# Two attention steps swapped on the matrix engine: new scores ahead of the older unit's probabilities times values

## The reference

```
x = x + tanh(g_xattn) * attention(layernorm(x), ctx)      # 16 heads of 64, causal
x = x + tanh(g_ffn)   * ffn(layernorm(x))                 # quantised gate/up/down products

attention(q, ctx):  qh, kh, vh = split_heads(q @ Wq, ctx @ Wk, ctx @ Wv)
                    p = softmax(mask(qh @ kh^T / 8));  out = (p @ vh) @ Wo + bo
```

## Time and profile before

| | before |
|---|---|
| three runs, median (lowest to highest) | 1842.2 us (1840.18 to 1842.58) |
| the profiled execution, its own time | 1842.63 us |
| its span from first to last instruction | 1840.6 us |
| PE busy in the span | 1722.7 us (94%) |
| DVE busy | 1375.7 us (75%) |
| ACT busy | 1128.3 us (61%) |
| POOL busy | 427.1 us (23%) |
| mean granted PE clock | 0.984 of full speed |

### The profile page before, as it was taken

The page is one execution under the profiler, slowest core; times in us unless marked ns, Lnnn a source line. Parts: engine busy times, 40 slices in busy tenths (PEclk is TensorE's granted clock), DMA queues, the critical chain, the costliest instruction groups (busy, mean ns, idle before and its releaser), DMA issues. The chain is left out here.

```text
span 1840.6 us, 36804 instructions
## 1 busy us (share of the span) xinstructions
PE 1722.7 (94%) x12200; PEld 1452.0 (79%) x12200; DVE 1375.7 (75%) x2260; ACT 1128.3 (61%) x3073; POOL 427.1 (23%) x373
## 2 busy tenths in 40 slices
PE   6899999999999999999999999959997887997998
PEld 5788888888888888888888887848885665786998
DVE  6667667677676676776766768758888998998785
ACT  4656566556566565565665655646656887664665
POOL 2222313323223232232232322210002332431000
PEclk9999999999999999999999999989998998998999
DMA  5010001000010011010100010016774563334664
GB/s 183 13 37 25 23 24 44 26 24 34 28 32 23 24 35 34 24 34 20 40 23 24 34 36 12 24 64 231 261 253 151 182 185 99 129 135 153 210 202 148
DMA packets 58600, 151.14 MB, mean 82 GB/s; under 512 B 4416, under 2 KB 33728, under 8 KB 56640
## 3 DMA queue, kind: packets, MB, share of 16 engines
q1 hardware_dynamic: 58560, 150.62, 24.3%
HBM read 85.07 MB, written 65.54 MB: 82 GB/s over the span
## 5 line engine op out<-in xcount | busy, mean ns | idle before, releaser
L320 POOL TENSOR_TENSOR prob<-prob,rsums 128x512 f32<-128x512 f32 x256 | 261.1, 1040 | 755.3 <-DVE rsums L497 755.3
L357 ACT ACTIVATE prob<-masked,neg_max 128x128 f32<-128x128 f32 x1024 | 396.0, 391 | 7.2 <-DVE neg_max L463 3.8
L368 ACT ACTIVATE qT<-proj 128x512 f32<-128x512 f32 x128 | 76.6, 598 | 260.9 <-PE proj L606 260.9
L479 DVE COPY probT<-trans 128x512 f32<-128x512 f32 x128 | 88.3, 690 | 152.6 <-PE trans L641 148.8
L357 ACT ACTIVATION_READ_ACCUMULATOR prob<-masked,neg_max 128x1 f32 x1024 | 195.6, 191 | 0.0
L463 DVE TENSOR_REDUCE neg_max<-masked 128x4 f32<-128x512 f32 x256 | 175.7, 686 | 8.8
L461 DVE TENSOR_TENSOR masked<-score,mask_add 128x512 f32<-128x512 f32 x256 | 174.1, 680 | 1.4 <-PE score L666 0.6
L758 PE MATMUL pair<-xThi,wup_hi 128*128 128x512 f32 x360 | 144.7, 402 | 28.4 <-POOL xTlo L1232 16.9
L641 PE MATMUL trans<-ident,prob 128*128 128x128 f32 x1024 | 153.3, 272 | 1.6 <-ACT probT L377 1.6
L677 PE MATMUL y<-wo_hi,o_hi 128*128 128x256 f32 x512 | 147.3, 288 | 3.6 <-DVE o_lo L503 3.6
L485 DVE COPY v_sb<-proj 128x512 f32<-128x512 f32 x128 | 88.5, 691 | 80.7 <-PE proj L606 80.0
(11 more groups left out here) (190 smaller groups left out, 4503.6 us busy)
## 6 DMA issues: line engine op xcount, KB each, us to landing
gate<-gate_d SPq DMA_DIRECT2D x30, 768.0 KB, 4.2
gate_d<-stage SPq DMA_DIRECT2D x8, 1536.0 KB, 6.0
n_u_d<-w_raw SPq DMA_DIRECT2D x16, 768.0 KB, 3.6
stage<-n_u_d SPq DMA_DIRECT2D x16, 768.0 KB, 5.9
gate_d<-gate SPq DMA_DIRECT2D x7, 1536.0 KB, 6.0
x_in<-in_x SPq DMA_DIRECT2D x16, 512.0 KB, 3.9
ctx_in<-in_ctx SPq DMA_DIRECT2D x16, 512.0 KB, 3.6
x_d<-x SPq DMA_DIRECT2D x16, 512.0 KB, 4.5
```

The costliest lines, as they stand in the source:

```text
L320: gp.tensor_tensor(pr, pr, rsums[:, h, :].rearrange("p (b o) -> p b o", o=1).broadcast_to([P, NB, P]), ALU.mult).then_inc(normed, 1)
L357: nc.scalar.activation(prob[:, c % 2, h, b, :], masked[:, h, b, :], ACT.Exp, bias=neg_max[:, h, b:b + 1], accum_out=psums[:, h, b:b + 1]). ...
L479: nc.vector.tensor_copy(probT[:, 1], trans[:]).then_inc(probT_copied[1], 1)
```

## The change

In PE's step, points 7 and 8 change places. Nothing else moves: the same instructions, waits and buffers, and the queues of ACT, DVE, POOL and SP keep their order.

```
@@ -718,10 +718,10 @@
                         value(g, i, n)
                 if nxt:
                     transpose_in(g, *ts[3])
+                if new:
+                    scores(g, c, u)
                 if old:
                     times_v(u - 2, co)
-                if new:
-                    scores(g, c, u)
 
             for n in range(2 * KC):
                 transpose_in(-1, first_job(n), n)
```

## The result

The changed kernel takes **1892.8 us** (median of four runs, 1888.83 to 1893.66) against 1841.6 before (four runs, 1840.18 to 1842.58): 1.0269 times as long, 95% interval 1.0255 to 1.0283. The forecast was 1879 with a range of 1870 to 1891, so the sign and the cause came out as written and the size did not: 51 us where the sum said 37. The profiled execution took 1893.66 us; its span is 1891.6, 51.0 more than before.

What follows compares the result with a forecast made beforehand. PE's queue was taken to bound the kernel. Fourteen repeated groups at 2.15 us (30.1) plus 6.5 for groups 0 and 15 gave 36.6 on 1842.63, so 1879 us, range 1870 to 1891.

Steps and rivals of the forecast that it cites:

- a stage is as long as PE's queue: Attention: PE is busy 94% of the span, so a change counts by what it does to that queue's waits.
- Earlier scores help nobody: Scores end 1.03 us earlier, but DVE's masks hardly wait for them; rival that this makes it faster, 1827, chance 0.04.
- The lateness of times_v: Each swapped unit: times_v ends 1.09 us later, delaying o_hi, o_lo and everything behind o_lo in DVE's queue.
- The seams at nothing: PE's switches between array splits around the two blocks: price taken as nothing, bounded at 7.6 us either way.
- xn at 1.37, not held: Unit 7: xn takes 1.37 us, not 2.06, as POOL is done; rival that the hold stays, 1889, chance 0.09.
- The clock at 1.00 in the repeated groups: Middle groups keep full clock; rival that new waits lower it in 15 groups, 24 us more, 1903, chance 0.07.
- no new wait is longer than about 1.5: Argument against the clock falling: PE's new waits stay at most about 1.5 us, against 3.4 where it fell.
- The late y: Units 1 to 5: the output projection's first weight load loses its head start, 0.07 us in each.
- PE's reaction to kT: Units 5 and 6: PE sees kT's end 0.05 us later; scores wait 0.57 and 1.00 us.
- The cover of unit 0: Unit 0: o_lo stands behind DVE's input copies, which hide the delay, so late y costs nothing there.
- its term: Unit 7: the first input transpose, waiting for xn, starts 1.87 us later, the total loss of units 5 to 7.
- Groups 0 and 15: Less slack because DVE also carries feed-forward weights: one and a half repeated groups, 3.2 us each, 6.5 together.

Runs made afterwards that it cites:

- e4: The swap only in units 5 and 6, the old order in all other units; 1866.7 us, 1.0132 of the kernel before.
- e3: The changed kernel with both layernorm statistics moved from behind o_lo to behind the masks of the next step; 1881.9 us, 1.021 of the kernel before.
- e11: The changed kernel with ACT's copy to kT ahead of head 0's four exponentials in units 5 and 6; 1874.7 us, 1.0181 of the kernel before.
- e9: The kernel before, unswapped, with earlier normalisation and the second layernorm's statistics in a DVE pause of unit 4; 1825.7 us, 0.991 of the kernel before.
- e10: The changed kernel with e9's moves, y behind the key projection and the masks' waits first in scores; 1835.2 us, 0.9956 of the kernel before.
- e2: The swap only in units 0 to 3 and 7, the old order in units 4 to 6; 1856.3 us, 1.0074 of the kernel before.
- e7: The changed kernel with the output projection (y) moved behind the key projection in units 0 to 5; 1884.2 us, 1.0224 of the kernel before.
- e1: The changed kernel with the masks' waits in scores put ahead of those for qT and kT; 1887.1 us, 1.0247 of the kernel before.

## Why the prediction was wrong in size and right in kind

**What held.** Steps that the runs bear out: a stage is as long as PE's queue. Earlier scores help nobody. The lateness of times_v reaches o_hi, o_lo, the statistics behind it, the masks, the exponentials, kT and then PE; e4 shows that it comes from the unit before, e3 that the statistics are a link of it, e11 that kT's place behind the exponentials is one. The seams at nothing: e9 and e10. xn at 1.37, not held: the changed trace, and POOL's pair ended 0.19 us ahead of xn. That was near the other way: in e3 and e11, where the pair overlaps xn again, the hold is back at 0.73 and 0.82. The clock at 1.00 in the repeated groups: the changed trace. The reason given for it, that no new wait is longer than about 1.5, did not hold in group 15, where kT kept PE for 2.35 us and the clock fell for 3.41. The late y at the start of units 1 to 5: e2 and e7.

**The term that failed first: PE's reaction to kT.** "PE sees it at 515.20 (0.05)" took the delay of a single wait, about what the transposes of unit 7 have (0.06). Behind the blocked wait of `scores` stand further entries, and each took about 0.1 us: 0.23 in unit 5 and 0.33 in unit 6 instead of 0.05. Units 5 and 6 came out 0.17 and 0.28 longer than predicted (0.81 for 0.64, 1.28 for 1.00), 14 x 0.45 = 6.3 us. e1, which moves the waits and nothing else, gave 0.17 and 0.19 of it back, 4.9 us in fourteen groups.

**The second: the late y.** It was put at 0.07 in units 1 to 4 and at nothing in unit 0, "which hide the delay". It measured 0.10, 0.09, 0.16 and 0.09 there, and 0.10 in unit 0, so 0.54 per group instead of 0.28: 14 x 0.26 = 3.6 us. e7 took the whole 0.54 away. The 0.09 to 0.10 is the load without its head start: the second matmul of y starts 0.21 us after the first and not 0.12. The 0.16 of unit 3 looks like the work of the residual, which stands ahead of o_lo on DVE in unit 2, but the rows of the changed kernel say otherwise:

```profile
506.19 1.40 DVE L562 SCALAR_TENSOR_TENSOR x<-y,tg,xres 128x512 f32<-128x512 f32 x2
...
508.34 0.69 DVE L503 TENSOR_TENSOR o_lo<-pv,o_hi 128x512 fp32r<-128x512 f32 x1 [0.60 <-ACT o_hi L395]
...
509.18 0.36 PE L677 MATMUL y<-wo_hi,o_hi 128*128 128x256 f32 x1
```

The residual ends at 507.59, and DVE then waits 0.60 us for o_hi; o_lo starts 1.77 us after its times_v (506.57), as in the other units. What unit 3 has more is a second wait in front of y (`wait_x1`): PE passes the wait for o_lo at 509.072, 0.04 after its end, and the load, which carries the other wait, starts at 509.149, 0.12 after o_lo's end, where it is 0.05 in unit 5 (526.88 to 526.93). So these 0.07 us are the first term's kind again, an entry more behind the blocked one.

The cover of unit 0, the input copies, was argued and not read from a row.

**The rest.** Unit 7 is 0.04 over its term (0.27 for 0.23), 0.6 us in all. Groups 0 and 15 cost 7.7 us and not 6.5; up to 1.7 of the 5.1 in group 15 are the 3.41 us at half clock, which the sum did not have. The 3.0 us behind the last q were not in the sum; 1.1 of them are the attention's own tail, up to 1.0 are more time at half clock, and whether these 1.0 and the 0.9 that are left belong to the change stays open, since the feed-forward stages vary by more. Together 6.3 + 3.6 + 0.6 + 1.2 + 3.0 = 14.7, against 51.0 - 36.6 = 14.4 that were missing (the unit medians are rounded).

**The range** ended at 1891 because it priced only what could go wrong with the seams, with xn and with two groups. The two terms that were off, 0.05 and 0.07, had no second value beside them: they looked too small to need one, but fourteen groups multiply them.

## What to carry to other kernels

Before an engine's step is put later, list all that stands behind its consumers in their queues. Here a microsecond on PE, by way of one copy on DVE, moved masks, exponentials and kT, and came back to PE twice in eight units, while the same swap cost nothing in the repeated groups once only slack work hung on that copy. When a cure takes a wait away, see what overlaps anew: in e3 and e11 xn met POOL's multiplications again, PE's wait for it grew from 1.11 to 1.85 and 1.95 us, and behind that wait the clock fell in four groups of fourteen. Put the wait that will be the last to be fulfilled last in the engine's queue, and count the waits behind a blocked one. Work that has time goes into a pause of its own engine, and into one where no neighbour with the same memory interface is busy: in e9 that, together with the earlier normalisation, made the kernel before 0.9% faster.

## What the runs showed that was not expected

A blocked wait on PE is followed by about 0.1 us for every further entry that PE passes on its way to the next load, even where the wait that it carries is long fulfilled (541.330, 541.436, 541.531, then the load at 541.616). A DVE instruction on 4 columns took 1.58 us and not 0.17 while POOL ran an addition of 2.41 us, and ended 0.02 us after it. The price of a seam did not depend on the order of the blocks: from value to scores, scores to times_v and times_v to q it is 0.33, 0.20 and 0.20 us from the last matmul of the one to the first of the other, the same as from value to times_v, times_v to scores and scores to q before.

The same wait can be followed by full or by half clock: PE waited 1.85 us for xn in every repeated group of e3 and 1.95 in every one of e11, and in four of the fourteen groups of each it then ran at 0.50 for 3.41 us, in the other ten at 1.00. The waits of 0.87 in the kernel before and of up to 1.24 in the changed one left the clock of all fourteen groups at 1.00.
